# Rows beyond an expert's first 128 in parts of 32, four experts' parts at once in four column strips

## The reference

```
logits = x @ router_w                      # 1600 rows, 14 experts
assignments = argmax(logits)               # one expert for a row
weights = softmax(logits)[assignments]
hid = gelu(x @ w1[e] + b1[e])              # w1: 14 x 256 x 512
out = (hid @ w2[e] + b2[e]) * weights      # w2: 14 x 512 x 256
x = layernorm(x + out)
```

## Time and profile before

| | |
|---|---|
| time, median of 3 runs | 519.66 us (518.99 to 521.2) |
| span of the profiled execution | 521.9 us |
| TensorE busy in the span | 476.3 us, 91% |
| blocks run in the last stage | 18 (288 records of L1742, 144 of L1753) |
| weight transfers of that stage issued after 440 us | 24 of 512 KB |

### The profile page before, as it was taken

How to read it: one execution, slowest core, us unless ns; L and a number is a source line. 1 busy time by engine, 2 the same in 40 slices (tenths; PEclk the granted TensorE clock), 3 DMA queues, 4 the chain that set the end, 5 groups by cost and what they waited for, 6 DMA issues and landing times. The chain is left out here.

```text
span 521.9 us, 12623 instructions
## 1 busy us (share of the span) xinstructions
PE 476.3 (91%) x4426; PEld 409.1 (78%) x4426; DVE 344.7 (66%) x960; ACT 306.5 (59%) x1402; POOL 216.0 (41%) x301
## 2 busy tenths in 40 slices
PE   3787789998999999989999989999999897999991
PEld 2475678886888888878878878788898687999981
DVE  1779658955788759895686788765666644455553
ACT  2356656777568778867387667666565822434330
POOL 1466444433444633544155255352243505144443
PEclk9999799998999999999999999999999887999996
DMA  5772134614051514524244105330011793999300
GB/s 167 194 174 40 48 128 167 214 62 146 13 193 31 177 34 171 183 68 161 84 147 155 51 25 170 114 107 22 21 33 46 234 368 128 344 375 374 110 26 17
DMA packets 43321, 69.45 MB, mean 133 GB/s; under 512 B 12199, under 2 KB 33432, under 8 KB 42539
## 3 DMA queue, kind: packets, MB, share of 16 engines
q1 hardware_dynamic: 39862, 39.45, 24.2%
q10 hardware_dynamic: 926, 25.83, 14.1%
q0 software_dynamic: 2464, 3.31, 2.1%
HBM read 58.71 MB, written 29.77 MB: 170 GB/s over the span
## 5 line engine op out<-in xcount | busy, mean ns | idle before, releaser
L1066 ACT ACTIVATE probs<-bank,neg_max 100x100 f32<-100x100 f32 x512 | 170.0, 371 | 37.2 <-DVE neg_max L1192 28.0
L970 POOL TENSOR_TENSOR probs<-probs,row_inv 100x400 f32<-100x400 f32 x128 | 111.6, 891 | 108.4 <-DVE row_inv L1197 108.1
L1066 ACT ACTIVATION_READ_ACCUMULATOR probs<-bank,neg_max 100x1 f32 x512 | 119.7, 234 | 0.0
L1192 DVE TENSOR_REDUCE neg_max<-bank 100x4 f32<-100x400 f32 x128 | 68.5, 563 | 13.6 <-PE bank L1538 7.5
L1549 PE MATMUL bank<-ident,probs 100*100 100x100 f32 x512 | 68.4, 257 | 7.2 <-POOL probs L970 4.2
L1549 PEld LDWEIGHTS bank<-ident,probs 100*100 100x100 f32 x512 | 50.9, 130 | 19.2 <-POOL probs L970 7.8
L1075 ACT COPY probsT<-bank 100x400 f32<-100x400 f32 x62 | 30.7, 496 | 43.8 <-PE bank L1549 38.1
L1204 DVE COPY probsT<-bank 100x400 f32<-100x400 f32 x66 | 37.6, 570 | 22.0 <-PE bank L1549 15.9
L1435 PE MATMUL bank<-yT,W_Q 128*128 128x250 f32 (+1 forms) x224 | 51.4, 373 | 0.4 <-DVE v_tile L1219 0.4
L1361 PE MATMUL bank<-cT_h,W_K 128*128 128x250 f32 (+1 forms) x224 | 46.5, 293 | 3.5 <-DVE kX L1120 1.8
L1797 ACT ACTIVATE hT<-bank,b1c 128x128 f32<-128x128 f32 x72 | 20.5, 368 | 38.8 <-PE bank L1742 38.8
(11 more groups left out here) (176 smaller groups left out, 974.4 us busy)
## 6 DMA issues: line engine op xcount, KB each, us to landing
expert_rows<-c_empty ACTq DMA_DIRECT2D x13, 1935.0 KB, 8.8
w<-in_L_ffn_w_dram SPq DMA_DIRECT2D x36, 512.0 KB, 9.9
vX<-v_tile SPq DMA_DIRECT2D x14, 200.0 KB
vX<-v_tile SPq DMA_DIRECT2D x12, 150.0 KB
xs<-in_x_dram SPq DMA_DIRECT2D x12, 125.0 KB
vX<-v_tile SPq DMA_DIRECT2D x12, 100.0 KB
kX<-in_L_xattn_WK_dram SPq DMA_DIRECT2D x2, 512.0 KB, 9.1
qX<-in_L_xattn_WV_dram SPq DMA_DIRECT2D x2, 512.0 KB, 6.1
```

The lines of the kernel that those rows point to most:

```text
L970: probs_ready.mark(pool.tensor_tensor(v, v, r, ALU.mult), step)
L1066: i = act.activation(probs[:, k % SLOTS, w], sc_bank[p % 2 * 2 + u][0:T, w], ACT.Exp, bias=neg_max[:, k % SLOTS, h:h + 1], accum_out=row_s ...
L1192: max_ready.mark(dve.tensor_reduce(neg_max[:, k % SLOTS, :], src, AX_X, ALU.max, negate=True), step)
```

## The change

- A part is now 32 rows (`SUB`) of one expert, and four parts (`LANES`), of up to four experts, form a group. The 128 rows of a group sit in one tile of 128 partitions, 32 for each part.
- In a group's fc1 the 32 rows of a part are stationary and that expert's w1 streams in 512 columns; the output of part j is partitions 32j to 32j+31 of one bank. So each matmul takes one column strip of TensorE (L1775). fc2 is done in the same way with 256 columns (L1798).
- The output of fc1 has rows on partitions, so the bias b1 comes as 32 rows of a tile `b1g`, is added by VectorE (`add_group_bias`), ScalarE does the gelu on 128x512 at once, TensorE turns the result back (`turn_h`, L1783, four transposes) and ScalarE copies it (`take_h`).
- The table of parts has 48 entries in place of 12. Two groups always run, at places 9 and 14 of the order; others, by pairs, behind a branch. The inputs give 2, 1, 3 and 2 parts for experts 0, 1, 10 and 13: eight parts, two groups, and no branch is taken.
- SyncE, for each part, reads two registers and issues three small transfers (rows, b1, b2), then for each part of a group both weights (1 MB). A group has eight weight transfers.

```diff
+    ORDER = [("block", n) for n in range(9)] + [("group", 0)] + [("block", n) for n in range(9, 13)] + [("group", 1), ("block", 13)]
...
+    WEIGHT_ORDER = [("block", n) for n in range(EARLY_WEIGHTS, 11)] + [("group", 0), ("block", 11), ("block", 12), ("group", 1), ("block", 13)]
...
+        def load_group(g):
+
+            if g >= 2:
...
+            for j in range(LANES):
+                m, lane = LANES * g + j, slice(SUB * j, SUB * (j + 1))
+                e = sp.value_load(expert_i[0:1, m:m + 1], min_val=0, max_val=NE - 1)
+                at = sp.value_load(home_i[0:1, m:m + 1], min_val=0, max_val=(NE + 1) * (CAP // SUB) - 1)
+                sp.dma_start(xg[lane, g % 2, :], parts_of_rows[bass.ds(at, 1)].rearrange("o r w -> r (o w)")).then_inc(group_in[g % 2], 16)
+                sp.dma_start(b1g[lane, g % 2, :], b1[bass.ds(e, 1), :].broadcast_to([SUB, F])).then_inc(group_in[g % 2], 16)
+                sp.dma_start(b2g[lane, g % 2, :], b2[bass.ds(e, 1), :].broadcast_to([SUB, D])).then_inc(group_in[g % 2], 16)
+
+        def load_group_weights(g):
+
+            sp.wait_ge(fc2_ready, group_weights(g)[-1] + 1)
...
+            for j, k in enumerate(group_weights(g)):
+                e = sp.value_load(expert_i[0:1, LANES * g + j:LANES * g + j + 1], min_val=0, max_val=NE - 1)
+                sp.dma_start(w1s[k][:, :, :], w1[bass.ds(e, 1)].rearrange("o (c p) f -> p (o c) f", p=P)).then_inc(group_w_in[g % 2], 16)
+                sp.dma_start(w2s[k][:, :, :], w2[bass.ds(e, 1)].rearrange("o (c p) d -> p (o c) d", p=P)).then_inc(group_w_in[g % 2], 16)
+
+        for kind, n in WEIGHT_ORDER:
+            if kind == "block":
+                sp.dma_start(w1s[n][:, :, :], w1[n].rearrange("(c p) f -> p c f", p=P)).then_inc(w_in[n], 16)
+                sp.dma_start(w2s[n][:, :, :], w2[n].rearrange("(c p) d -> p c d", p=P)).then_inc(w_in[n], 16)
+            else:
+                if n == 0:
+                    sp.wait_ge(more_ready, 3)
+                    for g in range(ALWAYS):
+                        load_group(g)
+                load_group_weights(n)
...
+                pe.wait_ge(group_w_in[n % 2], 2 * LANES * 16 * (n // 2 + 1))
+                pe.wait_ge(xT_taken, p + 1)
+                for c in range(KC):
+                    for j, k in enumerate(group_weights(n)):
+                        lane = slice(SUB * j, SUB * (j + 1))
+                        i = pe.matmul(h_bank[p % 2][lane, 0:F], xTs[:, p % SLOTS_X, c, lane], w1s[k][:, c, :],
+                                      start=(c == 0), stop=(c == KC - 1), skip_group_check=True)
...
+        for p, item in enumerate(ORDER):
+            fc1(item)
+            if p >= 1 and ORDER[p - 1][0] == "group":
+                turn_h(ORDER[p - 1][1])
+            for q in turned_after(p):
+                turn_x(ORDER[q])
+            if p >= 2 and ORDER[p - 2][0] == "group":
+                fc2(ORDER[p - 2])
+            if p >= 1 and ORDER[p - 1][0] == "block":
+                fc2(ORDER[p - 1])
```

More of the change, by code:

```diff
@@ L1757, in _ @@
             pe.matmul(y_bank[1][:, 0:P], ident[:, :], ident[:, :], start=True, stop=True)
[L1759 to L1764, removed]
-                if n > blocks[0]:
-                    fc2(n - 1)
-            fc2(blocks[-1])
-        run(list(range(ALWAYS)), turned_after)
+        for p, item in enumerate(ORDER):
[8 more added lines that the diff above has]
+                fc2(ORDER[p - 1])
+        if ORDER[-2][0] == "group":
+            fc2(ORDER[-2])
+        fc2(ORDER[-1])
         pe.wait_ge(more_ready, 3)
@@ L1772, in _, with take_x @@
             with pe.If(in_use(pe, first)):
-                for n in range(first, first + OB):
-                    turn_x(n)
-                run(list(range(first, first + OB)), lambda n: ())
+                for g in range(first, first + OB):
+                    turn_x(("group", g))
+                    fc1(("group", g))
+                    turn_h(g)
+                    fc2(("group", g))
     @block.scalar
     def _(act):
-        def take_x(n):
-            if n < INSERTED:
-                act.copy(xTs[:, n % SLOTS_X, 0, :], xT_bank[n][:, 0:P])
-                act.copy(xTs[:, n % SLOTS_X, 1, :], h_bank[n][:, 0:P]).then_inc(xT_taken, 1)
+        def take_x(item):
+            p = place_of[item]
+            if p < INSERTED:
+                act.copy(xTs[:, p % SLOTS_X, 0, :], xT_bank[p][:, 0:P])
+                act.copy(xTs[:, p % SLOTS_X, 1, :], h_bank[p][:, 0:P]).then_inc(xT_taken, 1)
@@ L1845, in _ @@
             with pool.If(in_use(pool, first)):
-                run(list(range(first, first + OB)))
+                for g in range(first, first + OB):
+                    finish(("group", g))
     @block.vector
@@ L1913, in _ @@
+        for p, item in enumerate(ORDER):
+            if item[0] == "group":
+                add_group_bias(item[1])
+            if p >= 2 and ORDER[p - 2][0] == "group":
+                finish(ORDER[p - 2])
+            if p >= 1 and ORDER[p - 1][0] == "block":
+                finish(ORDER[p - 1])
+        if ORDER[-2][0] == "group":
+            finish(ORDER[-2])
+        finish(ORDER[-1])
         for first in LATER:
             with dve.If(in_use(dve, first)):
-                run(list(range(first, first + OB)))
+                for g in range(first, first + OB):
+                    add_group_bias(g)
+                    finish(("group", g))
```

280 lines of the change are left out of this document (148 added, 132 removed).

## The result

The changed kernel takes 538.12 us (median of 4 runs, 536.59 to 539.63), the kernel before 520.43 in the same session (4 runs, 518.99 to 523.63). The ratio is 1.033, 95% interval 1.0287 to 1.0373: slower by 3.3%. Its profiled execution has a span of 537.9 us against 521.9.

What follows compares the result with a forecast made beforehand. TensorE set the pace before; SyncE's issuing of eight parts would now delay group 0's weights to 493.5. With 30.5 us of work and 2.5 of clock loss, the last fc2 moves 15.3: 519.7 + 15.3 = 535 us, range 525 to 543.

Steps and rivals of the forecast that it cites:

- SyncE's parts: SyncE ahead of group 0's weights: eight parts at 2.84 us each, 23.8 us in all, first weight issued at 479.2.
- near nothing: Sign in the DMA: its rate falls near zero from about 465 to 480 us.
- The wait: TensorE at place 9: group 0's weights land at 493.5, against an fc1 start of 475.59 before; 17.9 us of waiting.
- The clock: TensorE after the stall: the idle engine loses its clock, costing 2.5 us, between 0 and 3.3.
- The groups: TensorE: four strips fully overlapped, 4.8 us a group; TensorE alone would end some 5 us earlier.
- strips in turn: Rival on TensorE: serial 32-column passes, a group's fc1 and fc2 6.9 us each, 20.7 more, 556; chance 0.04.
- changes between strips and array: TensorE switching between strips and whole array: 0.15 us each, bounds 0 and 0.30, four a group.
- The end: Last fc2 ends at 526.5 against 511.2; VectorE's chains follow as before, so the end moves by 15.3 us.
- second stall: TensorE at group 1 and expert 13: weights land before they are needed, no stall, 3 us to spare.
- The sum: Whole kernel: 519.7 + 15.3 = 535 us, range 525 to 543.
- TensorE decides: Rival: weights in time and strips side by side, 519.7 - 5 = 514.5 us, faster; chance 0.02.
- the bytes decide: Rival: SyncE is cheap and DMA bytes set group 0's landing; stall 5 us, time 522; chance 0.04.

Runs made afterwards that it cites:

- the kernel without reload, nested: Changed kernel reading group weights where they lie, constant experts, later branches inside one another, parts issued earlier; 513.39 us, ratio 0.9868 to the kernel before.
- order-alone kernel: Changed kernel with only group 0 moved to place 11, behind blocks 9 and 10, parts still on SyncE; 537.45 us, ratio 1.0281 to before.
- order-by-landing kernel: Kernel with parts on ScalarE, plus group 0 at place 11 behind blocks 9 and 10 and parts at places 2 to 9; 520.35 us, ratio 0.999.
- the one where each weight has its own wait: Kernel with parts on ScalarE, but SyncE waits before each group weight for that buffer's own fc2, not the fourth's; 526.44 us, ratio 1.0107.

## Why the prediction was right, point by point

- **SyncE's parts.** 23.8 us forecast, 23.7 measured; the first group weight at 479.2 against 480.35 (the stage itself began 1.1 later). The total is closer than its terms, and that is luck: the shortest part took 2.62 (460.29 to 462.91), not 2.84, and the first transfers of the first parts took 0.40 and 0.32, not the 0.62 of a full queue; single slow steps, up to 1.33 for one transfer, made it up. That it is the issuing that costs is shown by the kernels with constant addresses and with the parts on ScalarE. The DMA rate from 465 to 480 was 82 GB/s, above the near nothing that I gave, since the small rows and the outputs still moved.
- **The wait.** 493.5 forecast for group 0's start, 494.12 measured; 17.9 us of idle forecast, 17.1 measured, with a weight transfer as its releaser.
- **The clock.** 1.2 GHz from 480.6 to 497.7; what it cost is the group's fc1, 3.57 against 1.86 from start to start, some 1.8 us with the transposes, inside the 0 to 3.3 given and below the 2.5 taken.
- **The groups.** Overlap was right and nearly full: 16 passes of 512 columns in 1.93 us, where a block's 16 passes over the whole array, with 128 columns each, take 1.95. From start to start a group's fc1 takes 1.86 against 1.79 and its fc2 1.86 (522.23 to 524.09) against 1.72, which is 3.7 times less than the 6.9 of strips in turn. The Trainium skill (TensorE: Matmul & The Clock Gate, Part 3) gives four row strips 3.07x and three column strips 2.38x; the rows here show more for four column strips, and the measurement decides. The changes between strips and array, taken at 0.15, are about 0.09 (513.66 to 515.48 is 1.82 against 1.73 of a plain fc2). The one makes up for the other: summed from start to start in the kernel without reload, nested, a group is some 4.7 us, with 4.8 forecast, and TensorE alone gains 5.1 to 5.3, with 5 forecast.
- **The end.** Last fc2 at 526.5 forecast, 526.08 measured. No second stall at group 1: its fc1 at 515.48 follows the fc2 ahead of it without a wait. In the order-alone kernel, whose first group weight is issued 0.6 earlier, group 1's weights released TensorE at 512.17, so the slack was about 2.7, with 3 forecast.
- **The sum.** 15.3 forecast as the shift of the last fc2, 14.9 measured in the profiles, of which 1.1 is the later start. The 13.7 left are the wait of 17.1 and the clock's 1.8, less some 5.2 that TensorE gains; the forecast had 17.9, 2.5 and 5. What the sum did not have: behind the last fc2 the end came 1.1 later than before, since TensorE's untaken branches, which I had not priced, run past ScalarE's tests, while VectorE's last chain began 1.10 us behind the last fc2 and not 1.86. The range of 525 to 543 holds 538.12; the 3 above the forecast are these 1.1, the start, and the spread of the runs (the kernel before itself came out at 520.43 in place of 519.66). That the excess stays this small is in part luck, as the wait and the clock were 1.5 below their terms.
- **The rivals.** "TensorE decides" and "the bytes decide" were rightly put low for this kernel. The second is what bounds it next: with the parts off SyncE the wait was 6.2 to 6.4 us, for which it had 5. So of the 17.1 us some 11 are issuing and 6 are bytes, as far as the kernels with the parts on ScalarE separate them: in them the DMA was full (376 GB/s) until group 0's weights were there. "Strips in turn" did not occur; where the program was made so, it cost 5.3 us in place of 20.7.

Left open: why the last stage begins up to 6 us earlier or later from profile to profile; it does so in all kernels here, and no run was made for it. The granted clock has a share in it. The 17 runs of the kernel before beside the order-by-landing kernel fall in two: seven with a mean clock of 0.959 to 0.963 took 522.1 to 523.9 us, ten with 0.968 to 0.978 took 518.5 to 520.4, but for one of 522.97. Why the clock differs from run to run is not shown.

## What to carry to other kernels

Price what an engine must do to issue a transfer, register reads and address arithmetic too, against what the DMA moves in that time: here 24 small transfers of 1 MB cost 24 us of a queue that moves 9 MB in them. Then look for the second bound before spending work on the first: reloading eight experts' weights for 8 parts of 32 rows takes more DMA time than the groups save TensorE, so that with the issuing moved to an engine that had time for it, and a better order, the change came out even, and only without the reload ahead. When a wait is long, look for its cause where the DMA rate fell, not where the engine stands.

## What the runs showed of the hardware that was not expected

- A branch that is not taken costs TensorE's queue a median of 2.8 us (0.35 to 3.1) where it jumps over the body of a pair of groups, and 3.34 where it jumps over all five at once; ScalarE, VectorE and GpSimd need about 0.05 for the latter (45 to 72 ns).
- Passes in other column strips are overlapped though they are not next in the program: with four passes of 512 columns to a strip, one strip after another, nothing is lost (1.95 us); with eight of 256 columns, 4.59 in place of 1.93. Whether the number or the length decides is not shown.
- A transfer with a constant address takes SyncE 0.46 us from start to start, so a part of three 1.4; with two registers read and worked with, a part takes 2.96 on average (2.62 at the least).
- The clock can fall behind short waits too: in the order-by-landing kernel 5.46 us of idle were followed by 3.64 us for the passes that take 1.92, and with group 1's parts later 2.69 us by 3.10. It need not: in the kernel with the parts on ScalarE the second wait, of 3.53 us, left the granted clock at 1.00, and the fc2 behind it took its 1.89; in the one where each weight has its own wait, 3.06 us were followed by an fc2 of 3.18.
